# Two running sums carried in the token rows: fused adds on VectorE in place of accumulating scatters

## The reference

```python
x = x + conv_block(_ln_c(x), ...)      # depthwise 3x3, ReLU, prune, 1x1, ReLU, prune
t = _to_tokens(x)                      # (16, 784, 128)
t = t + _L0_ffn_ref(_ln_t(t), ...)

# _L0_ffn_ref, E = 8 experts, F = 512, C = 1024 tokens each
probs = jax.nn.softmax(x_flat @ Wr, axis=0)
vals, idx = jax.lax.top_k(probs.T, C)            # every expert picks its 1024 tokens
h = gelu(selected @ W1 + b1);  out_e = h @ W2 + b2
output = zeros.at[idx.reshape(-1)].add(vals * out_e)
```

## Time and profile before

| | us |
|---|---|
| median of 3 runs (503.77 to 505.05) | 503.83 |
| profiled execution: span | 502.94 |
| profiled execution: around the span | 0.86 |
| PE busy / DVE busy / ACT busy / POOL busy | 361.9 / 327.1 / 274.3 / 159.3 |
| images: busy share of the DMA engines, 25 to 100 us and 100 to 195 us | 0.44 and 0.49 |

### The profile page before, as it was taken

How to read it: one execution, slowest core, us unless ns; L and a number is a source line. 1 busy time by engine, 2 the same in 40 slices (tenths; PEclk the granted TensorE clock), 3 DMA queues, 4 the chain that set the end, 5 groups by cost and what they waited for, 6 DMA issues and landing times. The chain is left out here.

```text
span 502.9 us, 6936 instructions
## 1 busy us (share of the span) xinstructions
PE 361.9 (72%) x1947; PEld 255.7 (51%) x1947; DVE 327.1 (65%) x1004; ACT 274.3 (55%) x587; POOL 159.3 (32%) x151
## 2 busy tenths in 40 slices
PE   4989888888889985631021798999990498876575
PEld 3656555566666553520011374677560467464453
DVE  5699988888889898578879548556620025235444
ACT  3577888888888876677640528556551240510000
POOL 4000000000000000000005777787888788876000
PEclk9999999999999997655555799999997598997755
DMA  4604555555554342479101223344443267847998
GB/s 103 188 38 141 185 168 185 167 185 168 185 182 150 130 131 96 137 238 392 71 1 33 55 56 94 95 65 64 83 85 34 55 189 134 194 61 169 285 390 344
DMA packets 36396, 72.01 MB, mean 143 GB/s; under 512 B 6385, under 2 KB 16785, under 8 KB 36369
## 3 DMA queue, kind: packets, MB, share of 16 engines
q1 hardware_dynamic: 24256, 56.52, 35.0%
q0 software_dynamic: 9472, 8.66, 11.2%
q10 hardware_dynamic: 2640, 6.51, 3.3%
HBM read 34.96 MB, written 30.29 MB: 130 GB/s over the span
## 5 line engine op out<-in xcount | busy, mean ns | idle before, releaser
L403 POOL DMA_INDIRECT picked<-token_rows,slot_idx x32 | 31.5, 986 | 270.7 <-issue 270.4
L691 PE MATMUL psC<-x_pad,tap_diag 128*128 128x392 f32 x256 | 90.8, 498 | 6.7 <-ACT x_pad L570 5.6
L1009 DVE SCALAR_TENSOR_TENSOR conv<-x_pad,taps_w,conv 128x784 f32<-128x784 f32 x64 | 65.9, 1030 | 0.8
L691 PEld LDWEIGHTS psC<-x_pad,tap_diag 128*128 128x128 f32 x256 | 46.1, 189 | 37.0 <-DVE conv L1009 5.1
L1302 DVE TENSOR_TENSOR y_sum<-psC,b_rows 128x512 f32<-128x512 f32 x15 | 10.4, 692 | 75.2 <-PE psC L869 75.2
L869 PE MATMUL psC<-w,hid 128*128 128x128 f32 x480 | 56.6, 280 | 2.2 <-ACT hid L633 2.1
L869 PEld LDWEIGHTS psC<-w,hid 128*128 128x128 f32 x480 | 55.8, 197 | 4.6 <-issue 3.0
L613 ACT ACTIVATE picked_T<-psA 128x512 f32<-128x512 f32 x16 | 9.0, 594 | 59.9 <-PE psA L836 59.9
L426 POOL DMA_INDIRECT moe_sum_late<-y_rows,slot_idx x24 | 37.9, 1581 | 9.5 <-issue 7.0
L483 ACT ACTIVATE rows<-psD,sm 112x128 f32<-112x128 f32 x98 | 35.7, 464 | 9.3 <-DVE sm L1001 9.3
L729 PE MATMUL psB<-act,pw_masked 128*128 128x392 f32 x64 | 27.9, 563 | 17.0 <-DVE pw_masked L1085 17.0
(11 more groups left out here) (211 smaller groups left out, 728.8 us busy)
## 6 DMA issues: line engine op xcount, KB each, us to landing
token_rows<-rows SPq DMA_DIRECT2D x16, 416.5 KB, 3.6
x_in<-in_x_dram SPq DMA_DIRECT2D x16, 392.0 KB, 3.5
x_res<-in_x_dram SPq DMA_DIRECT2D x16, 392.0 KB, 4.3
moe_sum<-zero_rows SPq DMA_DIRECT2D x16, 392.0 KB, 4.9
x_all<-x SPq DMA_DIRECT2D x16, 392.0 KB, 2.9
moe_sum_late<-zero_rows SPq DMA_DIRECT2D x16, 392.0 KB, 7.7
out_dram<-act ACTq DMA_DIRECT2D x16, 392.0 KB, 6.2
w<-in_L_ffn_W_dram SPq DMA_DIRECT2D x16, 256.0 KB, 3.3
```

Of the source, the lines that this page charges most:

```text
L403: nc.gpsimd.indirect_dma_start(out=picked_in[k][:, b, :], out_offset=None, in_=rows_dram, in_offset=bass.IndirectOffsetOnAxis(ap=slot_idx[ ...
L691: ins = nc.tensor.matmul(psC[:, h, 0:HALF].rearrange("c (h w) -> c h w", w=W), tap_diag[:, n, :], x_pad_v[:, q, y0:y0 + LINES, dx:dx + W], ...
L1009: return nc.vector.scalar_tensor_tensor(o, x_pad_v[:, q, y0 + dy:y0 + dy + lines, dx:dx + W], taps_w[:, PE_TAPS + n:PE_TAPS + n + 1], acc, ...
```

## The change

A token row in DRAM becomes WIDE = 392 floats (1568 bytes): sum A (128), the row as before (136), sum B (128). The image stage stores the sum fields as zeros with the rows, in pieces of 7 x 392 floats per partition, and the stores of zeros into moe_sum are gone. The rows' buffer in SBUF is cleared once for that by a memset of 5488 columns on GpSimd.

The experts form three chains. In chain 0 (experts 0, 2, 5) a gather takes sum A and the row, 264 floats; VectorE weighs and adds in one operation per block (four of 128 columns per half, in place of one of 512), and the scatter writes sum A back plainly. Chain 1 (1, 4, 6) does so with sum B. In both a gather waits until the scatter of the expert before it in its chain has landed. Chain 2 (3, 7) gathers 136 floats ahead of time into x_in and x_res, and scatters into moe_sum_late, expert 3 plainly and expert 7 with an add. Experts 2, 3, 5 and 6 (TURNED_LATE) are now turned half by half within themselves, where before they were turned ahead during the expert before. The slot work of expert 7 comes before that of expert 6 (SLOT_TURN).

There are 32 folds (FOLDS = 2 * B), 16 of sum A and 16 of sum B; each is loaded from token_rows in runs of 512 bytes where the loads of moe_sum had runs of 3584. They go by turns through psD and psA. The end, over moe_sum_late, is as before.

```diff
+WIDE = C + ROW + C
+X_AT, B_AT = C, C + ROW
+CHAINS = ((0, 2, 5), (1, 4, 6), (3, 7))
+TURNED_LATE = (2, 3, 5, 6)
+FOLDS = 2 * B
...
-            for img in range(B):
-                k = img % ENDS
-                if img >= ENDS:
-                    sp.wait_ge(s_fd, (img - ENDS) * 2 + 2)
+            for n in range(FOLDS):
+                chain, img, k = n // B, n % B, n % ENDS
+                if img == 0:
+                    sp.wait_ge(s_sca[chain], len(CHAINS[chain]) * (16 * SB))
+                if n >= ENDS:
+                    sp.wait_ge(s_fd, (n - ENDS) * 2 + 2)
+                at = (0, B_AT)[chain]
                 sp.dma_start(y_in[k].rearrange("p (t c) -> p t c", c=C),
-                             y_t[:, ds(img, 1), :, :].rearrange("p i t c -> p (i t) c")).then_inc(s_yf[k], 16)
-            sp.wait_ge(s_fd, 2 * B)
-
-            sp.wait_ge(s_sca[0], 16 * SB * E // 2)
-            sp.wait_ge(s_sca[1], 16 * SB * E // 2)
+                             rows_t[:, ds(img, 1), :, at:at + C].rearrange("p i t c -> p (i t) c")).then_inc(s_yf[k], 16)
+            sp.wait_ge(s_fd, 2 * FOLDS)
+            sp.wait_ge(s_sca[2], len(CHAINS[2]) * (16 * SB))
...
-            nc.gpsimd.memset(zero_rows[:, :], 0.0)
+            nc.gpsimd.memset(zero_rows, 0.0)
+            nc.gpsimd.memset(rows[:, :, :], 0.0)
...
             def gather(e, half):
-                k = e % BUFS
-                if e >= BUFS and half == 0:
-                    pool.wait_ge(s_pt, (e - BUFS) * 2 + 2)
-                    pool.wait_ge(s_ge, e - BUFS + 1)
-                pool.wait_ge(s_idx, e * 2 + (half + 1))
+                k, turn = buffer_of(e)
+                if k < 2 and turn and half == 0:
+                    pool.wait_ge(s_sca[k], turn * (16 * SB))
+                pool.wait_ge(s_idx, SLOT_TURN.index(e) * 2 + half + 1)
...
             def scatter(e):
-                q = e % 2
-                if e == SECOND:
+                chain, turn = chain_of(e)
+                if e == CHAINS[2][0]:
                     pool.wait_ge(s_lz, 16 * B)
-                elif e >= 1:
-                    pool.wait_ge(s_sca[1 - q], (e + 1) // 2 * (16 * SB))
-                if e == SECOND + 1:
-                    pool.wait_ge(s_sca[q], SECOND // 2 * (16 * SB))
-                sums = y_dram if e < SECOND else late_dram
+                if e == CHAINS[2][1]:
+                    pool.wait_ge(s_sca[2], 16 * SB)
...
+                    if chain < 2:
+                        nc.gpsimd.indirect_dma_start(out=rows_dram, out_offset=at, in_=weighted(e)[:, b, :], in_offset=None,
+                                                     element_offset=(0, B_AT)[chain]).then_inc(s_sca[chain], 16)
...
-            def weigh(e, q, use, h):
+            def weigh(e, h):
                 dve.wait_ge(s_gt, e + 1)
                 dve.wait_ge(s_yb, e * 2 + h + 1)
-                if since(e, 2):
-                    dve.wait_ge(s_sca[q], use * (16 * SB))
...
+                for b in range(4 * h, 4 * h + 4):
+                    ins = nc.vector.scalar_tensor_tensor(weighted(e)[:, b, :], y_sum[:, b, :], gate[:, b:b + 1],
+                                                         weighted(e)[:, b, :], ALU.mult, ALU.add)
+                ins.then_inc(s_yr, 1)
```

More of the change, by code:

```diff
@@ L205, in build, with buffer_of, weighted @@
         y_rows = sb("y_rows", [128, 2, SB, C])
+        def buffer_of(e):
+            chain, turn = chain_of(e)
+            return (chain, turn) if chain < 2 else (2 + turn, 0)
+        def weighted(e):
+            k, _ = buffer_of(e)
+            return picked_y[k] if k < 2 else y_rows[:, k - 2, :, :]
         y_in = [ln_tok[:, 0, :], ln_tok[:, 1, :], x_pad[0:P, 0, 0:TPI * C], x_pad[0:P, 1, 0:TPI * C]]
@@ L653, in expert @@
                         gelus(e, h)
-                if e == E - 2:
-                    take_turned(e + 1, 0)
-                elif e < E - 2:
+                if e + 1 < E and e + 1 not in TURNED_LATE:
                     for h in range(2):
@@ L859, in hidden @@
                     if f in after:
-                        after[f](2 if e == 0 else e + 3)
+                        after[f](2 if e == 0 else SLOTS_AHEAD[e])
             def down(e, q, h):
@@ L892, in first_expert, with expert @@
                     turn_picked(1, h)
-            def expert(e, q, use, ahead, another):
+            def expert(e, q, use):
                 pe.wait_ge(s_w1[q], use * 16 + 16)
                 for h in range(2):
-                    if isinstance(e, int) and e == E - 1 and h == 1:
-                        for img in range(4, 7):
-                            turn_first(img)
+                    if e in TURNED_LATE:
                         turn_picked(e, h)
-                    slot_work = ({2: first_ties}, {1: slot_ranks})[h] if ahead else {}
+                    slot_work = ({2: first_ties}, {1: slot_ranks})[h] if e in SLOTS_AHEAD else {}
                     hidden(e, q, h, slot_work)
-                late = isinstance(e, int) and e == E - 2
-                if another and not late:
+                if e + 1 < E and e + 1 not in TURNED_LATE:
                     for h in range(2):
@@ L928, in _ @@
             for e in range(1, E):
-                expert(e, e % 2, e // 2, e + 3 < E, e + 1 < E)
-            for img in range(7, B):
-                turn_first(img)
-            pe.wait_ge(s_fk, 2 * B)
+                expert(e, e % 2, e // 2)
+            for n in range(4, FOLDS):
+                turn_sums(n)
+            pe.wait_ge(s_fk, 2 * FOLDS)
             pe.wait_ge(s_gelu, E * 2 * FT)
@@ L1313, in expert @@
-            def expert(e, q, use, ahead):
-                if ahead:
-                    slots_a(e + 3)
-                    slots_b(e + 3)
-                    slots_c(e + 3)
-                    slots_d(e + 3)
+                k, _ = buffer_of(e)
+                if k >= 2:
+                    nc.vector.tensor_tensor(weighted(e)[:, 4 * h:4 * h + 4, :], y_sum[:, 4 * h:4 * h + 4, :],
+                                            gate[:, 4 * h:4 * h + 4].unsqueeze(2).to_broadcast([128, 4, C]), ALU.mult).then_inc(s_yr, 1)
+                    return
```

223 lines of the change are left out of this document (119 added, 104 removed).

## The result

The changed kernel takes 530.76 us (median of 4 runs, 527.38 to 532.15), the kernel before beside it 504.43 (503.77 to 505.05): a ratio of 1.0501, 95% interval 1.0458 to 1.0544. It is slower by 5%; the forecast was 521.6, with a range of 506 to 536. The profiled execution has a span of 530.0 us; it was the longest of the four. One execution of a later kernel (eight buffers and products, 528.37 us where its others took 519.56 to 521.25) fell in a slower state of the chip and is left out of its ratio.

A forecast was written before the change was run, and what follows sets the result against it. TensorE was taken to pace the experts up to expert 5, then gathers behind GpSimd's adding scatters. Experts ending at 437.0, 28 folds to 481.8 and 38.96 of end gave a 520.8 us span, forecast 521.6, range 506 to 536.

The forecast's parts named there:

- Start: Kernel start: the added memset of 5488 columns delays slot_col and then VectorE; +1.5 us carried through, bounds 0 and 1.7.
- a wide gather at the price of a bare one: Expert stage, GpSimd: a gather of 1056-byte rows takes 0.99 us, as with 544-byte rows; GpSimd's work falls 24 us.
- Late-turned experts: Expert stage: an expert turned half by half within itself takes 18.5 us against 16.7.
- Folds: After expert 7: 28 folds at 1.6 us, 44.8 us, mainly TensorE at its lower clock; last turned at 481.8.
- lower DMA bound of 0.97: Fold loads: 401 KB at the 415 GB/s that zero stores reached takes 0.97 us; the upper bound was 1.74.
- two rules weighed: Fold loads: 512-byte transfers reach line rate, 0.97 us a load; against it, runs starting off a 256-byte boundary cost extra beats.
- Start of the third sum: End of kernel: the sync queue starts the third sum only when all 32 folds are turned; 38.96 us follow.
- folds at VectorE's pace: Rival, late folds: 1.07 us each, TensorE's clock stays up, loads hidden; 506.8 us, chance 0.12.
- Wide gathers at the price of adding ones: Rival, expert stage: wide gathers cost 1.86 us instead of 1.26, 28.8 us more GpSimd work; 540 us, chance 0.12.
- Closing experts: Rival, expert stage: experts 1 to 6 take 16.7 us or less each, folds 1.07; 491 us, chance 0.07.
- Faster: Outcome for the whole kernel: it beats the kernel before, by the experts overlapping well; chance 0.07.

The follow-up runs named there:

- eight buffers and products: Changed kernel with eight buffers for fold loads instead of four, and a 384-column TensorE product ahead of each of the 28 last folds; ratio 1.0303.

## Why the prediction was right, and where its steps were not

The mechanism held: GpSimd's saving is real and off the path, and 28 folds stand in one unbroken stretch at the end, with 38.9 us behind them. By its own terms the span was to be 520.8 and was 530.0:

- **Start**, 1.5 predicted, 5.1 in this execution. The step took the clearing for a delay of slot_col alone. It also blocks VectorE (tap_diag came at 10.59, as predicted, yet image 0's residual sum was 2.7 us late), some 2 us in all at the first gather, and 3 more us belong to a clock that varies by run. 3.6 us of miss.
- **GpSimd**: a wide gather at the price of a bare one, 0.957 us. Right.
- **Late-turned experts**, 18.5 predicted, 18.8 with slot work: 19.1 from expert 2's turn to expert 3's (327.22 to 346.35). From the first gather to the 28 folds it was 172.2 us, where the working had 168.3 (437.0 less the 268.65 of a first gather 1.5 us late): 3.8 us of miss, the sum of misses both ways. Expert 2 was turned 1.7 us late (expert 1 took 17.8 us for 15.9, and the wait of 2 us behind it was 0.27), expert 6 waited 4.36 us for its gather for the 2.6 of the working, and took 21.3 us for 18.5, since its first products ran at 1.2 GHz (3.78 us for 1.98). Against that expert 7 took 18.4 us for 20.6: its four folds cost 4.0 us and not four times 1.5. That they cancel in part is luck.
- **Folds**, 28 at 1.6: 28 at 1.67, 1.9 us of miss. The reason was wrong, and that the size was nearly right is luck. I named TensorE at the lower clock; it is the loads in 512-byte pieces, priced by the working at 0.97 to 1.74 us. TensorE's 1.57 lies just under their 1.64 to 1.73, so the trace of after alone, with TensorE 93% busy, reads as if TensorE were the bound, though the DMA share of 1.06 stands in the same row. Only taking its work or its low clock away, with nothing gained, told them apart. The lower DMA bound of 0.97 came from stores; loads never came near it. Of the two rules weighed in "DMA: Bandwidth & Descriptors" of the Trainium skill, the first, that 512 bytes reach line rate, gave the wrong pace for these loads (1.64 us and more, where it had 0.97, and where runs of 3584 bytes took 1.36 to 1.45). The second points the right way. Whether the length, the spacing or the rows' position off a 256-byte boundary costs it was not tried, so the first may still hold for aligned runs.
- **Start of the third sum** only after all 32 folds, 38.9 us of end: right.

3.6, 3.8 and 1.9 make 9.3 us, the 9.2 between 520.8 and 530.0 but for rounding.

The rivals: folds at VectorE's pace fell as a steady pace; the 0.95 us that eight buffers showed for thirteen folds is what it needs, loads in stock, and less than the 1.07 of the working. Wide gathers at the price of adding ones fell (0.957 us and 0.3 of issue, for 1.86). Closing experts fell with 19.1. "Faster" was one sum field away: what decided the sign was the second field's folds, 29 us. Against them GpSimd's 24 us less of work let the experts end only 9.6 us sooner after the first gather (172.2 us for 181.8).

## To carry to other kernels

Where two resources need nearly the same time for a step, the busier row does not name the bound; take work away from one and see whether the pace moves, and read the DMA share beside the engines. Price a transfer by a row of the same direction and run length, and count buffers as a stock that must be filled while something else runs. A clearing on GpSimd is not free cover: check what VectorE has to do in that time, and clear only what is read.

## What the runs showed of the hardware

- VectorE operations of 0.16 to 0.2 us stood for up to 2.82 us behind GpSimd's clearing, and 2.08 us behind 28 clearings of 128 columns each (0.19 us, one begun every 0.15 us): nothing got in between them.
- TensorE with transposes alone had a granted clock of 1.2 GHz at 93% busy (13.94 of 15 us); with one product of 384 columns between folds, 2.4 GHz at 90% (13.43 of 15).
- Loads of 392 KB: 224 to 240 GB/s in 512-byte runs, whatever TensorE did and with four or eight buffers; 299 in runs of 3584 bytes with eight, 255 to 263 with four.
- A gather of 1056-byte rows cost GpSimd what one of 544 bytes did, 957 ns; the adding scatter's landing took 3.3 to 3.4 us with no other loads and 5.9 to 6.5 beside the folds' loads.
